# The first pair of x through DRAM and 32-by-32 block transposes, u by one matmul, w from two fp32r halves, in a fused attention and FFN kernel

## The chip, the cores and the metric

The kernel runs on one core of one Trainium2 chip. The metric is the device time of one execution in microseconds, lower is better. The profile is one execution of the program taken by the hardware profiler; its clock starts at the span's start.

## What is computed

Eight sequences of 256 rows and 1024 features, all float32:

```python
x = x + attn(layernorm(x), ctx, Wq, bq, Wk, bk)   # softmax((xn Wq^T + bq)(ctx Wk^T + bk)^T / 32) ctx
x = x + layernorm(x) @ weights + bias             # weights rebuilt from 4-bit codes, scales and zeros
```

The kernel folds the two projections: it makes M = Wq^T Wk once, and then t = xn M for all rows, so that scores are t ctx^T. The biases give two vectors: u = Wk^T bq, which is added to t per column, and w = Wq^T bk, whose product with each row of xn is a term of that row. Float32 products are made of two fp32r halves each (hi and lo, lo = full - hi) with three matmuls: hi hi, hi lo, lo hi.

## The kernel before

All engines run their own written-out programs and meet at semaphores. TensorE's order is: 24 warming transposes, the projection M in eight blocks of 128 rows (`proj(b, c)`, b the block, c the contraction slice, six matmuls of 128x512 each, 48 a block; blocks 0 and 1 are interleaved), then t in four pairs of batches (`for p in range(PAIRS)`, `for j in range(NB)`, n = 8 p + j, 24 matmuls of 128x512 each), with eight `gather` steps of the FFN's tables behind n = 4, 6, 9, 11, 16, 18, 22, 24; then scores, softmax, the product with ctx, and the FFN.

Around each projection block b, ScalarE splits block b + 1 of Wq (`wq_split(b + 1, 0)` after slice 3 of block b has been used, since there is one buffer; `wq_split(b + 1, 1)` after the whole of block b), multiplies block b by bk (`times_bk(b)`, eight instructions) and copies M's hi half (two `m_hi`). VectorE makes the lo halves of the same (`wq_split`, `m_lo`) and sums the products with bk into `wacc` (`sum_bk(b)`). SyncE's queue loads Wq's blocks through three stages: `load_wq(b)` waits until `times_bk(b - 3)` is done.

Layer norm of batches 0 and 1 is on VectorE in blocks 4 and 5: `x_stats` (four bn_stats) and `x_apply` in place in `xin`. In block 7 TensorE transposes them: `x_tr(u)`, four 128x128 float32 transposes of each of eight u into banks 6 and 7, from where ScalarE (`x_hi(0, u)`) and VectorE (`x_lo(0, u)`) write `xT_hi` and `xT_lo` over Wk's halves, once slice 3 of block 7 is used. `u_sums`, behind slice 6 of block 7, sums `uacc` over the partitions with eight float32 matmuls against a column of ones, each two instructions in the trace, and one more for bq bk. `w_row`, behind block 7, sums `wacc` over the partitions with two float32 matmuls of 128x512 (four instructions). ScalarE copies its result four times (`wrow`, `wrow_q`); then VectorE does `row_terms(0)`, `row_terms(1)`, `x_stats(2)`, `x_apply(2)`, `row_terms(2)`, `x_stats(3)`, `x_apply(3)`, `row_terms(3)` and `pick(0)`, which makes the one-hot table that the first gather waits for.

Batches 2 to 7 already take another way: applied rows are written to `xin` with their columns reordered (`by_quadrant`), stored to DRAM in rows of 4 KB (`store_xn`), reloaded in 1 KB pieces so that each 32 partitions hold one quarter of the features (`load_quadrants`, four DMAs on ScalarE's queue), and transposed in place in 32-by-32 blocks by VectorE (`x_blocks`, 128x2048). The first matmul of pair p waits for `x_lo(p, 0)`. For n = 0 the i-th contraction step also waits for the halves of M's block i.

Of the kernel before, what the change touches and what calls it, by code (L numbers as in the profile page):

```python
# [13 lines left out]
P = 128  # L14
# [34 lines left out]
def xattn_ffn_kernel(nc, x, ctx, Wq, bq, Wk, bk, qweight, qzeros, scales, bias, g_idx, out):  # L49
# [21 lines left out]
    with ExitStack() as stack:  # L71
# [49 lines left out]
        qz = at("qz", 200.25, [P, P], I32)  # L121
        KT = QUADRANTS[-1] + G
# [24 lines left out]
        xq = [None] + [at(f"xq{p}", kb, [P, 2 * NB, S], F32) for p, kb in ((1, slot[2]), (2, slot[4]), (3, 162.25))]  # L147
# [11 lines left out]
        xjunk = [at(f"xjunk{t}", 188.25 + 2 * t, [P, D], BF16) for t in range(QT)]  # L159

# [41 lines left out]
        s_const, s_small = sem("constants_made"), sem("small_loaded")  # L202
        s_placed = sem("table_placed")
# [22 lines left out]
        s_xraw, s_xst = [sem(f"raw_x_loaded{i}") for i in range(2)], sem("xn_stored")  # L226
        s_xql = [sem(f"xn_reloaded{i}") for i in range(2)]
        s_xT = sem("xn_transposed_by_blocks")
        s_xtr, s_xhi, s_xlo = sem("xn_transposed"), sem("xT_hi_done"), sem("xT_lo_done")
# [90 lines left out]


# [14 lines left out]
        def _(sp):  # L336
# [88 lines left out]
            def load_raw(b):  # L425
                if b == 2:
                    sp.wait_ge(s_m, 2 * NB)
                elif b == 3:
                    sp.wait_ge(s_xtr, NB)
# [104 lines left out]
        def _(pool):  # L534
# [9 lines left out]

            pool.wait_ge(s_tab[1], 16 * len(QUADRANTS))
# [8 lines left out]
            def rsqrt(n):  # L554
                if n < KH:
                    pool.wait_ge(s_stat, n + 1)
                elif n < B:
                    pool.wait_ge(s_xsq, QT * (n - KH + 1))
                    pool.tensor_scalar(mv[:, :, 1], xsquares, 1.0 / D, EPS, ALU.mult, ALU.add).then_inc(s_xvar, 1)
                    pool.wait_ge(s_xvar, n - KH + 1)  # L560
                else:
                    pool.wait_ge(s_stat, n - B + KH + 1)
                if n < KH:
                    pool.tensor_tensor(rstd, mv[:, :, 1], power, ALU.pow).then_inc(s_rstd, 1)
                else:
                    pool.tensor_tensor(rstd, mv[:, :, 1], power, ALU.pow).then_inc(s_rpow, 1)
                    pool.wait_ge(s_rpow, n - KH + 1)
# [57 lines left out]
        def _(act):  # L625
# [55 lines left out]

            def x_hi(p, u):
                if p == 0:
                    act.wait_ge(s_xtr, u + 1)
                    act.wait_ge(s_wqused, NB)
                    copy(xT_hi[:, u, :], bank[6 + u % 2][:, :]).then_inc(s_xhi, 1)
                else:
                    act.wait_ge(s_xT, 2 * p)
                    if u < NB - 1:
                        act.wait_ge(s_xused, (NB - 1) * (p - 1) + u + 1)  # L690
                    else:
                        act.wait_ge(s_t, NB * p)
                    copy(xT_hi[:, u, :].rearrange("p (m j) -> p m j", j=32), xq[p][:, :, 32 * u:32 * u + 32]
                         ).then_inc(s_xhi, 1)

            for b in range(NB):
# [19 lines left out]
            x_hi(0, 6)  # L716
            x_hi(0, 7)
# [52 lines left out]
            def load_quadrants(b):  # L770
                act.wait_ge(s_xst, 16 * (b - 1))
                if b == B - 1:
# [5 lines left out]

            def x_stats(b):
                act.wait_ge(s_xraw[b % 2], 16 * (b // 2))  # L780
                if b == KH:
                    act.wait_ge(s_placed, 16 * 8)
                    act.wait_ge(s_xn, QT * KH)
                for t in range(QT):
                    act.activation(xjunk[t], raw_rows(b)[:, t, :], ACT.Copy, accum_out=xsum[:, t:t + 1]).then_inc(s_xsum, 1)
                act.wait_ge(s_xsum, QT * (b - KH + 1))
                act.activation(nmean, xsum, ACT.Copy, scale=-1.0 / D).then_inc(s_xmean, 1)
                act.wait_ge(s_xmean, b - KH + 1)
                for t in range(QT):
                    act.activation(xjunk[t], raw_rows(b)[:, t, :], ACT.Square, bias=nmean[:, t:t + 1],  # L790
                                   accum_out=xsquares[:, t:t + 1]).then_inc(s_xsq, 1)

            def x_apply(b):
                act.wait_ge(s_rstd, b + 1)
                act.wait_ge(s_xst, 16 * (b - 2))
                act.wait_ge(s_dot, b)
                for t in range(QT):
                    act.activation(by_quadrant(xin[:, 1, t, :]), raw_rows(b)[:, t, :].rearrange("q (k a i) -> q k a i", k=NB, a=4),
                                   ACT.Identity, bias=shift[:, t:t + 1], scale=rstd[:, t:t + 1]).then_inc(s_xn, 1)
# [128 lines left out]
        def _(dve):  # L928
# [82 lines left out]
            def x_stats(b):  # L1011
                if b < 2:
                    dve.wait_ge(s_xl[b], 16)
                    ln_stats(xin[:, b, :, :])
                else:
                    dve.wait_ge(s_xraw[b % 2], 16 * (b // 2))
                    ln_stats(raw_rows(b))

            def x_apply(b):
                dve.wait_ge(s_rstd, b + 1)  # L1020
                if b == 2:
                    dve.wait_ge(s_xtr, NB)
                elif b > 2:
                    dve.wait_ge(s_xst, 16 * (b - 2))
                for t in range(QT):
                    if b < 2:
                        out_, in_ = xin[:, b, t, :], xin[:, b, t, :]
                    else:
                        out_, in_ = by_quadrant(xin[:, 1, t, :]), raw_rows(b)[:, t, :].rearrange("q (k a i) -> q k a i", k=NB, a=4)
                    dve.tensor_scalar(out_, in_, mv[:, t, 0:1], rstd[:, t:t + 1], ALU.subtract, ALU.mult).then_inc(s_xn, 1)  # L1030

            def x_blocks(b):
                dve.wait_ge(s_xql[b % 2], 64 * (b // 2))
# [3 lines left out]
            def x_lo(p, u):  # L1037
                dve.wait_ge(s_xhi, NB * p + u + 1)
                if p == 0:
                    low(xT_lo[:, u, :], bank[6 + u % 2][:, :], xT_hi[:, u, :], s_xlo)  # L1040
                else:
                    low(xT_lo[:, u, :].rearrange("p (m j) -> p m j", j=32), xq[p][:, :, 32 * u:32 * u + 32],
                        xT_hi[:, u, :].rearrange("p (m j) -> p m j", j=32), s_xlo)

            def copy_u():
                dve.wait_ge(s_u, 1)
                dve.tensor_copy(ucol, bank[4][:, 0:2 * NB].rearrange("p (j two) -> p j two", two=2)[:, :, 0]
                                ).then_inc(s_cons, 1)
                order.link(dve.tensor_copy(bsum[:, 1:2], bank[4][:, 2 * NB:2 * NB + 1]))
# [3 lines left out]
            for b in range(NB):  # L1053
# [13 lines left out]
                if b == NB - 1:  # L1067
                    for u in range(5):
                        x_lo(0, u)
                    copy_u()  # L1070
                    x_lo(0, 5)
# [8 lines left out]
            x_lo(0, 6)  # L1080
            x_lo(0, 7)
# [253 lines left out]
        def _(pe):  # L1335
# [5 lines left out]
            def x_tr(u):  # L1341
                pe.wait_ge(s_xn, 4)
                wait(pe, s_xlo, u - 1)
                for bt in range(2):
                    for t in range(QT):
                        o = bt * S + t * P
                        ins = pe.transpose(bank[6 + u % 2][:, o:o + P], xin[:, bt, t, u * P:(u + 1) * P], ident)  # L1347
                ins.then_inc(s_xtr, 1)

            def u_sums():  # L1350
                pe.wait_ge(s_uacc, NB - 1)
                pe.wait_ge(s_mlo, 2 * (NB - 2))
                for j in range(NB):
                    pe.matmul(bank[4][:, 2 * j:2 * j + 2], uacc[:, j * P:(j + 1) * P], ones2, start=True, stop=True)
                pe.wait_ge(s_cons, 1)
                pe.matmul(bank[4][:, 2 * NB:2 * NB + 2], bsum[:, 0:1].broadcast_to([P, P]), ones2,
# [39 lines left out]
            def w_row():  # L1396
                pe.wait_ge(s_wacc, NB)
                pe.wait_ge(s_cons, 3)
# [191 lines left out]
```

## Time and profile before

| | us |
|---|---|
| median of 3 runs | 547.49 (547.34 to 547.99) |
| the profiled execution | 547.35 |
| its span on the core | 545.6 |
| TensorE busy | 539.3 (99%) |
| VectorE busy | 372.4 (68%) |
| ScalarE busy | 268.0 (49%) |
| GpSimd busy | 187.2 (34%) |

The profiled execution took 547.35, its span 545.6; the other 1.75 lie around it. Matmuls are pipelined, so the duration printed for one (0.39) is longer than the distance to the next; distances between starts are what counts.

### The profile page before, as it was taken

The page shows a single profiled execution, that of the slowest core. Times are in us where ns is not written, and L with a number is a line of the kernel's source. Part 1 is how long each engine was busy: PE and PEld are TensorE (multiplying, and loading weights), DVE is VectorE, ACT ScalarE, POOL GpSimd, SP SyncE. Part 2 cuts the span into 40 slices and gives each one's busy share as a digit, 9 for nine tenths or more (in the row PEclk, how much of TensorE's full clock was granted, in tenths as well). Part 3 has the DMA queues.
Part 4 walks back from the last instruction along what each step waited for, and adds up shares of the span by engine and source line. Part 5 has one row for each costly group of instructions (what it writes and reads, how often), then busy time and mean ns, then how long its engine had stood idle before and what let it go on. Part 6 is the DMA issues. An engine that isn't in the chain of part 4 may idle for free.

```text
span 545.6 us, 7455 instructions
## 1 busy us (share of the span) xinstructions
PE 539.3 (99%) x2686; PEld 452.0 (83%) x2686; DVE 372.4 (68%) x616; ACT 268.0 (49%) x474; POOL 187.2 (34%) x147
## 2 busy tenths in 40 slices
PE   8999999999999999999999999999999999999997
PEld 7888888887777877778898999998788888888886
DVE  4989775787698774793424555574768779778742
ACT  6983444414767582343437766686563243324210
POOL 1072000010011000000326877777756644753530
PEclk9999999999999999999999999999999999999999
DMA  8942100359688756836384899898346775774311
GB/s 270 314 157 79 38 1 0 123 156 313 195 228 292 204 193 193 262 86 192 126 293 144 298 362 355 321 389 346 144 123 244 220 216 203 230 232 134 98 77 77
DMA packets 56036, 108.14 MB, mean 198 GB/s; under 512 B 12000, under 2 KB 32552, under 8 KB 53824
## 3 DMA queue, kind: packets, MB, share of 16 engines
q1 hardware_dynamic: 49472, 101.38, 54.1%
q10 hardware_dynamic: 6528, 6.29, 5.7%
q8 instruction: 21, 0.34, 0.3%
q14 instruction: 15, 0.12, 0.1%
HBM read 67.74 MB, written 39.85 MB: 197 GB/s over the span
## 4 chain that ended last, share of the span: by engine, by line
PE 86%; DVE 4%; ACT 3%; DMA 3%; issue 1%; POOL 1%; ACTq 0%; SPq 0%; DVEq 0%; POOLq 0%
PE bank L1337 22%; PE bank L1339 22%; PE bank L1338 22%; PE bank L1384 5%; PE bank L1390 5%; PE bank L1387 5%; PE bank L1438 2%; DMA xq<-xn_scratch 1%; ACT yin L868 1%; POOL cn_lo L578 1%; DVE xq L1035 1%; DMA wq_stage<-in_L_xattn_Wq 1%; DVE xT_lo L932 1%; PE bank L1347 1%; ACT cn_hi L627 1%
## 5 line engine op out<-in xcount | busy, mean ns | idle before, releaser
L1337 PE MATMUL bank<-xT_hi,m_hi 128*128 128x512 f32 x256 | 101.0, 395 | 0.0
L1339 PE MATMUL bank<-xT_hi,m_lo 128*128 128x512 f32 x256 | 99.7, 390 | 0.0
L1338 PE MATMUL bank<-xT_lo,m_hi 128*128 128x512 f32 x256 | 99.6, 389 | 0.0
L585 POOL TENSOR_TENSOR tT_lo<-t_pair,tT_hi 128x1024 fp32r<-128x1024 f32 x16 | 38.1, 2398 | 75.4 <-ACT tT_hi L627 75.4
L1289 DVE TENSOR_TENSOR xres<-xres,bank 128x512 f32<-128x512 f32 x56 | 38.3, 683 | 36.1 <-PE bank L1339 36.0
L599 POOL TENSOR_TENSOR l_lo_s<-l_sum_s,l_hi_s 128x512 fp32r<-128x512 f32 x32 | 40.4, 1297 | 56.0 <-DVE l_sum_s L1230 56.0
L824 ACT ACTIVATE t_pair<-bank,ucol 128x512 f32<-128x512 f32 x32 | 22.0, 687 | 74.1 <-PE bank L1339 69.6
L1337 PEld LDWEIGHTS bank<-xT_hi,m_hi 128*128 128x128 f32 x256 | 48.0, 188 | 11.8 <-issue 2.1
L1339 PEld LDWEIGHTS bank<-xT_hi,m_lo 128*128 128x128 f32 x256 | 48.0, 188 | 10.2
L1338 PEld LDWEIGHTS bank<-xT_lo,m_hi 128*128 128x128 f32 x256 | 48.1, 188 | 10.0 <-issue 0.2
L1384 PE MATMUL bank<-wk_hi,wq_hi 128*128 128x512 f32 x128 | 50.5, 394 | 0.2 <-DVE wq_lo L932 0.2
L1390 PE MATMUL bank<-wk_hi,wq_lo 128*128 128x512 f32 x128 | 49.9, 390 | 0.0
L1387 PE MATMUL bank<-wk_lo,wq_hi 128*128 128x512 f32 x128 | 49.8, 389 | 0.0
L578 POOL TENSOR_TENSOR cn_lo<-cin,cn_hi 128x512 fp32r<-128x512 f32 x32 | 40.3, 1289 | 26.0 <-ACT cn_hi L627 26.0
L932 DVE TENSOR_TENSOR cT_lo<-bank,cT_hi 128x512 fp32r<-128x512 f32 x32 | 20.7, 686 | 28.6 <-ACT cT_hi L627 28.4
L605 POOL TENSOR_TENSOR xres<-xres,bias_rows 128x1024 f32<-128x1024 f32 x16 | 38.3, 2398 | 0.0
L1337 PE MATMUL bank<-r_tile,l_hi_s 128*128 128x512 f32 x96 | 37.4, 390 | 0.0
L1339 PE MATMUL bank<-r_tile,l_lo_s 128*128 128x512 f32 x96 | 37.4, 389 | 0.0
L1338 PE MATMUL bank<-r_tile,l_hi_s 128*128 128x512 f32 x96 | 37.4, 389 | 0.0
L627 ACT ACTIVATE l_hi_s<-l_sum_s 128x512 fp32r<-128x512 f32 x32 | 20.3, 634 | 34.2 <-DVE l_sum_s L1226 16.2
L1337 PE MATMUL bank<-cT_hi,tT_hi 128*128 128x256 f32 x128 | 36.6, 286 | 0.0
L1339 PE MATMUL bank<-cT_hi,tT_lo 128*128 128x256 f32 x128 | 35.7, 279 | 0.0
(158 smaller groups left out, 1244.0 us busy)
## 6 DMA issues: line engine op xcount, KB each, us to landing
xres<-in_x SPq DMA_DIRECT2D x8, 1024.0 KB, 11.9
out<-xres SPq DMA_DIRECT2D x15, 512.0 KB, 5.2
right_scratch<-part_hi SPq DMA_DIRECT2D x28, 256.0 KB, 2.2
cin<-in_ctx SPq DMA_DIRECT2D x7, 1024.0 KB, 6.1
xn_scratch<-xin SPq DMA_DIRECT2D x6, 1024.0 KB, 4.7
xq<-xn_scratch ACTq DMA_DIRECT2D x24, 256.0 KB, 5.4
r_tile<-right_scratch SPq DMA_DIRECT2D x6, 1024.0 KB, 12.2
yn_scratch<-yin SPq DMA_DIRECT2D x6, 1024.0 KB, 4.0
```

Of the source, the lines that this page charges most:

```text
L578: pool.tensor_tensor(cn_lo[:, kt, cols], cin[b % 3][:, kt, cols], cn_hi[:, kt, cols].bitcast(F32), ALU.subtract).then_inc(s_cnlo, 1)
L585: pool.tensor_tensor(tT_lo[b][:, ks, :], t_pair[b // 2][:, b % 2, ks, :], tT_hi[b % 2 if b else 2][:, ks, :].bitcast(F32), ALU.subtract).t ...
L599: pool.tensor_tensor(l_lo[name], l_sum[name], l_hi[name].bitcast(F32), ALU.subtract).then_inc(s_llo_p, 1)
L605: pool.tensor_tensor(x1_of(f)[:, t, :], x1_of(f)[:, t, :], bias_rows, ALU.add).then_inc(s_rb, 1)
L932: return dve.tensor_tensor(out_, full, hi.bitcast(F32), ALU.subtract).then_inc(done, 1)
L1289: dve.tensor_tensor(part, part, prod_bank(f, n)[:, :], ALU.add).then_inc(s_acc, 1)
L1337: pe.matmul(out_, a_hi, b_hi, start=start, stop=False, skip_group_check=True)
L1338: pe.matmul(out_, a_hi, b_lo, start=False, stop=False, skip_group_check=True)
L1339: return pe.matmul(out_, a_lo, b_hi, start=False, stop=stop, skip_group_check=True)
L1384: pe.matmul(out_, q_hi, wk_hi[:, c, cols], start=c == 0, stop=False, skip_group_check=True)
L1387: pe.matmul(out_, q_hi, wk_lo[:, c, cols], start=False, stop=False, skip_group_check=True)
L1390: ins = pe.matmul(out_, q_lo, wk_hi[:, c, cols], start=False, stop=c == NB - 1, skip_group_check=True)
```

## The change

- `x_stats` and `x_apply` of batches 0 and 1 move from VectorE (blocks 4 and 5) to ScalarE (blocks 3 and 4): two Copy with a sum, the mean, two Square with a sum, GpSimd's rsqrt and shift, two Identity in place. `x_stats` stands between `wq_split(b + 1, 0)` and `times_bk(b)`, `x_apply` behind `wq_split(b + 1, 1)` and ahead of `m_hi(b)`.
- Each batch is stored to DRAM by SyncE's queue as eight DMAs with 128-byte pieces on the SBUF side (`store_first`), and reloaded by four DMAs (`reload_first`). `store_first(0)` stands ahead of `load_wq(7)`; behind that stand `reload_first(0)`, `store_first(1)`, `reload_first(1)`.
- VectorE transposes them by blocks in blocks 6 and 7; `x_hi` and `x_lo` of pair 0 read `xq[0]` as those of other pairs do, all eight ahead of M's block 7. `x_tr` is gone.
- u: VectorE transposes `uacc` by blocks and sums over 32 columns in block 4 (`upart`); one float32 matmul of 32 columns against `same` (ones where partition and column agree modulo 32; made by GpSimd at the start) and the one for bq bk follow, behind slice 6 of block 4.
- w: `wacc` is split into `w_hi` (ScalarE) and `w_lo` (VectorE) at block 7, and `w_row` is four fp32r matmuls of 128x512.

```diff
             for b in range(3, NB):
+                if b == NB - 1:
+                    store_first(0)
                 sp.wait_ge(s_wqlo, wq_split_count(b - 3, 1))
                 sp.wait_ge(s_wqbk, b - 2)
                 load_wq(b)
...
+            reload_first(0)
+            store_first(1)
+            reload_first(1)
...
+            def store_first(b):
+                sp.wait_ge(s_xn, QT * (b + 1))
+                for t in range(QT):
+                    pieces = xin[:, b, t, :].rearrange("p (k a i) -> p a k i", k=NB, a=4)
+                    for a in range(4):
+                        sp.dma_start(xn_dram[b, t * P:(t + 1) * P, a * S:(a + 1) * S].rearrange("p (k i) -> p k i", k=NB),
+                                     pieces[:, a, :, :]).then_inc(s_xst0[b], 16)
+
+            def reload_first(b):
+                sp.wait_ge(s_wklo, NB)
+                sp.wait_ge(s_wkbq, NB)
+                sp.wait_ge(s_xst0[b], 16 * 4 * QT)
+                rows = xn_dram[b].rearrange("(m j) f -> j m f", j=32)
+                for a in range(4):
+                    sp.dma_start(xq[0][32 * a:32 * a + 32, b * NB:(b + 1) * NB, :], rows[:, :, a * S:(a + 1) * S]
+                                 ).then_inc(s_xq0[b], 16)
...
@@ ScalarE
                 elif 1 < b < NB - 1:
                     wq_split(b + 1, 0)
+                    if b in (3, 4):
+                        x_stats(b - 3)
                     times_bk(b)
                     wq_split(b + 1, 1)
+                if b in (3, 4):
+                    x_apply(b - 3)
                 if b == NB - 1:
-                    for u in range(6):
+                    act.wait_ge(s_const, 3)
+                    copy(ones_r, ones2)
+                    act.wait_ge(s_wacc, NB)
+                    copy(w_hi, wacc).then_inc(s_whi, 1)
+                    for u in range(NB):
                         x_hi(0, u)
...
@@ VectorE
-                if b in (4, 5):
-                    x_stats(b - 4)
-                    x_apply(b - 4)
+                if b == KH:
+                    dve.wait_ge(s_uacc, NB - 1)
+                    order.link(dve.transpose(uacc, uacc))
+                    dve.tensor_reduce(upart, uacc.rearrange("p (b i) -> p b i", i=32), AX_X, ALU.add).then_inc(s_upart, 1)
+                if b == 5:
+                    copy_u()
+                if b >= NB - 2:
+                    x_blocks(b - (NB - 2))
...
                 if b == NB - 1:
-                    for u in range(5):
+                    dve.wait_ge(s_whi, 1)
+                    low(w_lo, wacc, w_hi, s_wlo)
+                    for u in range(NB):
                         x_lo(0, u)
...
@@ TensorE
             def u_sums():
-                pe.wait_ge(s_uacc, NB - 1)
-                pe.wait_ge(s_mlo, 2 * (NB - 2))
-                for j in range(NB):
-                    pe.matmul(bank[4][:, 2 * j:2 * j + 2], uacc[:, j * P:(j + 1) * P], ones2, start=True, stop=True)
+                pe.wait_ge(s_upart, 1)
+                pe.wait_ge(s_same, 1)
+                pe.matmul(bank[7][:, 0:32], same, upart, start=True, stop=True)
...
                 for h in range(2):
-                    pe.matmul(bank[4 + h][:, :], ones2[:, 0:1].broadcast_to([P, P]), wacc[:, h * HALF:(h + 1) * HALF],
-                              start=True, stop=True).then_inc(s_wr, 1)
+                    cols = slice(h * HALF, (h + 1) * HALF)
+                    pe.matmul(bank[4 + h][:, :], ones, w_hi[:, cols], start=True, stop=False, skip_group_check=True)
+                    pe.matmul(bank[4 + h][:, :], ones, w_lo[:, cols], start=False, stop=True, skip_group_check=True
+                              ).then_inc(s_wr, 1)
...
                     proj(b, c)
+                    if b == 4 and c == 6:
+                        u_sums()
                     if b == NB - 1:
-                        if c == 6:
-                            u_sums()
-                        for u in {3: (0, 1), 4: (2,), 5: (3, 4), 6: (5,), 7: (6, 7)}.get(c, ()):
-                            x_tr(u)
                         if c == NB - 1:
                             w_row()
```

## Rows read from the trace of the kernel before

**Rows 1.** The page, busy time by engine and TensorE's granted clock in tenths.

```profile
PE 539.3 (99%) x2686; PEld 452.0 (83%) x2686; DVE 372.4 (68%) x616; ACT 268.0 (49%) x474; POOL 187.2 (34%) x147
...
PEclk9999999999999999999999999999999999999999
```

**Rows 2.** TensorE's timeline, end of the projection: start, duration, engine, line, operation, tiles.

```profile
87.92 0.39 PE L1390 MATMUL bank<-wk_hi,wq_lo 128*128 128x512 f32 x1
88.15 1.03 PE L1347 MATMUL bank<-ident,xin 128*128 128x128 f32 x8
...
89.25 0.40 PE L1387 MATMUL bank<-wk_lo,wq_hi 128*128 128x512 f32 x1
...
94.50 1.84 PE L1354 MATMUL bank<-pairs,uacc 128*128 128x2 f32 x16
...
96.42 0.63 PE L1347 MATMUL bank<-ident,xin 128*128 128x128 f32 x4
...
98.29 1.03 PE L1347 MATMUL bank<-ident,xin 128*128 128x128 f32 x8
99.16 1.88 PE L1400 MATMUL bank<-wacc,pairs 128*128 128x512 f32 x4
...
101.11 0.39 PE L1338 MATMUL bank<-xT_lo,m_hi 128*128 128x512 f32 x1
```

**Rows 3.** TensorE's timeline, around the first gather and the start of pair 1.

```profile
127.89 0.39 PE L1339 MATMUL bank<-xT_hi,m_lo 128*128 128x512 f32 x1
128.21 0.39 PE L1426 MATMUL bank<-tab,onehot 32*128 32x512 bf16 x4
...
145.36 0.39 PE L1339 MATMUL bank<-xT_hi,m_lo 128*128 128x512 f32 x1
```

**Rows 4.** ScalarE's timeline: block 3, block 6, then statistics and their application to batch 4.

```profile
44.88 0.63 ACT L627 ACTIVATE wq_hi<-wq_stage 128x512 fp32r<-128x512 f32 x1 [3.53 <-PE bank L1390]
45.42 2.45 ACT L655 ACTIVATE wq_bk<-wq_stage,bcols 128x128 f32<-128x128 f32 x8
...
84.46 2.46 ACT L655 ACTIVATE wq_bk<-wq_stage,bcols 128x128 f32<-128x128 f32 x8
...
101.67 0.62 ACT L627 ACTIVATE uacc<-bank 128x512 f32<-128x512 f32 x1
...
131.72 1.06 ACT L785 ACTIVATE xjunk<-xin 128x1024 bf16<-128x1024 f32 x1 [2.71 <-DMA xin<-in_x]
...
136.47 0.67 ACT L824 ACTIVATE t_pair<-bank,ucol 128x512 f32<-128x512 f32 x1
137.93 2.38 ACT L798 ACTIVATE xin<-xin,shift,pairs 128x1024 f32<-128x1024 f32 x2 [0.78 <-POOL shift L568]
```

**Rows 5.** VectorE's timeline: the last sum_bk, the row terms, pick(0), pair 1's lo halves.

```profile
86.95 1.97 DVE L979 TENSOR_REDUCE wacc<-wq_bk 128x128 f32<-128x1024 f32 x1 [1.43 <-ACT wq_bk L655]
...
102.33 0.69 DVE L1090 CUSTOM_DVE_ANT_0 junk<-xin,wrow 128x512 f32<-128x512 f32 x1 [1.32 <-ACT uacc L627]
...
127.14 0.33 DVE L1105 TENSOR_SCALAR onehot<-gid,pid 128x128 bf16<-128x128 bf16 x1
...
141.07 2.31 DVE L1035 STREAM_TRANSPOSE xq<-xq 128x2048 f32<-128x2048 f32 x1 [7.06 <-DMA xq<-xn_scratch]
...
144.59 4.90 DVE L932 TENSOR_TENSOR xT_lo<-xq,xT_hi 128x512 fp32r<-128x512 f32 x8
```

**Rows 6.** Groups of VectorE instructions by shape: busy us, mean ns, idle before.

```profile
L1035 DVE STREAM_TRANSPOSE xq<-xq 128x2048 f32<-128x2048 f32 x6 | 13.8, 2308 | 13.0 <-DMA xq<-xn_scratch 13.0
L945 DVE TENSOR_TENSOR wk_lo<-wk_stage,wk_hi 128x1024 fp32r<-128x1024 f32 x5 | 6.1, 1223 | 1.5 <-ACT wk_hi L627 1.5
L1193 DVE TENSOR_REDUCE pairs<-bank 128x2 f32<-128x512 f32 x8 | 5.5, 682 | 0.0
```

**Rows 7.** DMA issue timelines, then two-microsecond windows: length, busy by engine, clock, DMA share, GB/s.

```profile
240.23 6.16 SPq L459 DMA_DIRECT2D cq<-in_ctx  x4
...
118.80 1.85 ACTq L776 DMA_DIRECT2D xq<-xn_scratch  x4
...
116.00:118.00 2.00, 2.00 (x11) 1.65 (x10) 1.86 (x8) 0.56 (x1) 0.00 (x0) 1.00 1.01 403
244.00:246.00 2.00, 2.00 (x10) 1.66 (x9) 1.86 (x4) 0.00 (x0) 0.00 (x0) 1.00 0.74 114
246.00:248.00 2.00, 2.00 (x11) 1.65 (x10) 1.21 (x3) 0.60 (x2) 0.00 (x0) 1.00 0.96 151
```

More of the change, by code:

```diff
@@ L121, in xattn_ffn_kernel @@
         qz = at("qz", 200.25, [P, P], I32)
+        same = at("same", 200.75, [P, P], F32)
+        upart = at("upart", 206.5, [P, 32], F32)
+        ones_r = at("ones_r", 206.625, [P, 2], F32R)
+        w_hi = at("w_hi", 196.25, [P, D], F32R)
+        w_lo = at("w_lo", 192.25, [P, D], F32R)
         KT = QUADRANTS[-1] + G
@@ L159, in xattn_ffn_kernel @@
         xjunk = [at(f"xjunk{t}", 188.25 + 2 * t, [P, D], BF16) for t in range(QT)]
+        xjunk_early = [at(f"xjunk_early{t}", 61.75 + 2 * t, [P, D], BF16) for t in range(QT)]
         cn_hi = at("cn_hi", 178.25, [P, QT, D], F32R)
@@ L319, in xattn_ffn_kernel @@
                 LO_AT.setdefault(SUMS[k] + i // 2, []).append((k, i))
+        ON_ACT = {b: i + 1 for i, b in enumerate((0, 1, 4, 5, 6, 7))}
         X_STATS = {1: 3, 5: 4, 10: 5, 12: 6, 17: 7}
@@ L543, in _ @@
             pool.iota(pidi, [[0, 1]], base=0, channel_multiplier=1).then_inc(s_const, 1)
+            order.link(pool.memset(same, 0.0))
+            for d in range(-3, 4):
+                ins = pool.affine_select(out=same, in_=same, compare_op=ALU.not_equal, fill=1.0,
+                                         base=32 * d, pattern=[[-1, P]], channel_multiplier=1)
+                if d < 3:
+                    order.link(ins)
+            ins.then_inc(s_same, 1)
             pool.wait_ge(s_tab[1], 16 * len(QUADRANTS))
@@ L680, in _, with x_stats @@
                 times_bq(c)
+            def x_stats(b):
+                if b < 2:
+                    act.wait_ge(s_xl[b], 16)
+                    rows, places = xin[:, b, :, :], xjunk_early
+                    if b == 0:
+                        act.wait_ge(s_uacc, NB - 1)
+                else:
+                    act.wait_ge(s_xraw[b % 2], 16 * (b // 2))
+                    rows, places = raw_rows(b), xjunk
+                    if b == KH:
+                        act.wait_ge(s_placed, 16 * 8)
+                        act.wait_ge(s_xn, QT * KH)
+                for t in range(QT):
+                    act.activation(places[t], rows[:, t, :], ACT.Copy, accum_out=xsum[:, t:t + 1]).then_inc(s_xsum, 1)
+                act.wait_ge(s_xsum, QT * ON_ACT[b])
+                act.activation(nmean, xsum, ACT.Copy, scale=-1.0 / D).then_inc(s_xmean, 1)
+                act.wait_ge(s_xmean, ON_ACT[b])
+                for t in range(QT):
+                    act.activation(places[t], rows[:, t, :], ACT.Square, bias=nmean[:, t:t + 1],
+                                   accum_out=xsquares[:, t:t + 1]).then_inc(s_xsq, 1)
@@ new lines, in x_apply @@
+            def x_apply(b):
+                act.wait_ge(s_rstd, b + 1)
+                if b >= 2:
+                    act.wait_ge(s_xst, 16 * (b - 2))
+                    act.wait_ge(s_dot, b)
+                for t in range(QT):
+                    if b < 2:
+                        out_, in_ = xin[:, b, t, :], xin[:, b, t, :]
+                    else:
+                        out_, in_ = by_quadrant(xin[:, 1, t, :]), raw_rows(b)[:, t, :].rearrange("q (k a i) -> q k a i", k=NB, a=4)
+                    act.activation(out_, in_, ACT.Identity, bias=shift[:, t:t + 1], scale=rstd[:, t:t + 1]).then_inc(s_xn, 1)
@@ L1011, in x_stats @@
             def x_stats(b):
[L1012 to L1017, printed above, removed]
+                dve.wait_ge(s_xraw[b % 2], 16 * (b // 2))
+                ln_stats(raw_rows(b))
             def x_apply(b):
@@ L1038, in x_lo @@
                 dve.wait_ge(s_xhi, NB * p + u + 1)
[L1039 to L1043, printed above, removed]
+                low(xT_lo[:, u, :].rearrange("p (m j) -> p m j", j=32), xq[p][:, :, 32 * u:32 * u + 32],
+                    xT_hi[:, u, :].rearrange("p (m j) -> p m j", j=32), s_xlo)
             def copy_u():
                 dve.wait_ge(s_u, 1)
-                dve.tensor_copy(ucol, bank[4][:, 0:2 * NB].rearrange("p (j two) -> p j two", two=2)[:, :, 0]
-                                ).then_inc(s_cons, 1)
-                order.link(dve.tensor_copy(bsum[:, 1:2], bank[4][:, 2 * NB:2 * NB + 1]))
+                for a in range(4):
+                    rows = slice(32 * a, 32 * a + 32)
+                    ins = dve.tensor_copy(ucol[rows, :], bank[7][rows, 0:32].rearrange("p (k a) -> p a k", a=4)[:, a, :])
+                ins.then_inc(s_cons, 1)
+                order.link(dve.tensor_copy(bsum[:, 1:2], bank[7][:, 32:33]))
                 dve.sem_inc(s_cons, 1)
```

99 lines of the change are left out of this document (34 added, 65 removed).

## The prediction

> **What bounds the kernel now.** I read busy time by engine first: TensorE is busy 539.3 of 545.6 us at full clock throughout [rows 1], so a microsecond of TensorE work taken out is worth a microsecond only if nobody else becomes late. Next TensorE's own timeline where the change acts. Matmuls of 128x512 start 0.227 us apart: from the second one of t at 101.11 to the last ahead of the first gather at 127.89 there are 118 steps, 26.78 us [rows 2, 3]. So a projection block of 48 takes 10.88 us, and with slice 4 of block 7 due at 88.15 the earlier blocks begin at 50.07 (block 4), 60.95 (5), 71.83 (6) and 82.71 (7). Last I read VectorE's and ScalarE's timelines for where they stand relative to TensorE [rows 4, 5], and this decides the forecast: the first gather (128.21) needs the one-hot table, made from 127.14 to 127.47, only 0.7 us ahead; and the first matmul of pair 1, due 0.227 behind that of 145.36, needs the lo half made from 144.59, ready at 145.28, so 0.1 us or so is spare. Both hang on one chain that starts with VectorE's row terms at 102.33.
>
> **TensorE's work: what goes.** The 24 matmuls left of block 7 would end, and t start, at 88.15 + 5.44 = 93.59. The second matmul of t starts at 101.11, so the first effectively at 100.88. The extras cost 7.3 us by that, or summed from the gaps: eight transposes push the next pair of matmuls by 89.25 - (88.15 + 0.23) = 0.87, that is 0.109 each, 3.5 for 32; the 18 instructions for u 94.50 to 96.42, 1.9; w 99.16 to 100.88, 1.7. Sum 7.1 to 7.3 [rows 2].
>
> **What comes.** w: four fp32r matmuls of 512 columns, 4 x 0.227 = 0.9. u: two float32 matmuls, four instructions at 1.92/18 = 0.107, so 0.43. Net work taken off TensorE: 7.2 - 1.3 = 5.9 us. If TensorE stayed the only bound this would be the gain.
>
> **ScalarE in blocks 3 and 4 (times of the trace of before).** Statistics of a batch cost 4.75 (131.72 to the next instruction at 136.47), an application 2.3 (137.93, two in 2.38 with their overlap) [rows 4]. Block 3: wq_split(4, 0) at 44.88, next 45.42; statistics to 50.17; times_bk(3), 2.35 to the next instruction, to 52.5; wq_split(4, 1) to 53.1; application to 55.4; m_hi(3) to 56.3. Block 4: wq_split(5, 0) to 56.9, statistics to 61.6, times_bk(4) to 63.9, wq_split(5, 1) to 64.5, application to 66.8. VectorE follows: sum_bk(3) 52.6 to 54.55 (as 86.95, 1.97 [rows 5]), lo of wq_split(4, 1) at 55.25. TensorE needs that for slice 4 of block 4 at 55.51: cover of 0.2 us, so a stall of 0 to 0.3, and I take 0.05.
>
> **u on VectorE.** Its transpose and sum come behind m_lo(3) (waits for m_hi(3), so 56.0 to 57.2) and lo of wq_split(5, 0) (to 57.8). No row shows either at this size: the transpose of 2048 columns takes 2.31, a sum of 512 0.68 [rows 6]; for 1024 columns I take 1.2 each by halving and doubling; the ends are 0.7 and 2.0 (sum_bk's strided 1024 [rows 5]) for the sum. So upart is ready at 60.4. TensorE reaches the end of slice 6 of block 4 at 50.07 + 7 x 1.36 + 0.05 = 59.6. It stalls 0.75 (0.2 to 1.6), with everything behind it queued. With 0.05, the work of 0.43 and a drained pipeline of 0.1 TensorE is delta = 1.3 us later than before from block 5 on. Were that stall absent, slice 4 of block 5 would bind instead: its lo half is ready at 66.6 against 66.4 + 0.5, so delta is not under 0.5. With delta = 1.3 this has 1.1 us of cover.
>
> **SyncE's queue.** load_wq(6) now waits for the later times_bk(3): 52.6 instead of 47.9, lands by 57, needed at 67. store_first(0) starts at 55.4 ahead of load_wq(7); that waits for times_bk(4) at 63.9 anyway and lands by 69, needed at 79. How long the store takes is the unknown that matters. 1 MB in 128-byte pieces is moved once in this trace, from DRAM for cq: four issues fill 6.16 us (240.23 to 246.4), with 4.9 from the last issue to landing at most, and the engines carry 114 to 151 GB/s then against 403 for xn in 4 KB rows [rows 7]. So the ends are 4.7 (as the 4 KB rows) and, in the other direction, an unknown above the 9.6 of cq; I take 9.6, the same piece size. A reload takes 1.85 of issue and some 5.4 to land, 7.3 [rows 7]. Then: store(0) 55.4 to 65, reload(0) to 72.4 (needed at 80), store(1) from 67, sharing with the reload, to 79.5, reload(1) to 86.8. VectorE asks for it at 88.86 + 1.3 = 90.2. Hidden, with 3.4 us of cover. load_raw(2) behind it waits for block 7's end, later than that.
>
> The Trainium skill speaks against this edit: "DMA: Bandwidth & Descriptors", in its opening table, says that transfers need 512 B or more for line rate because the engine below that does a read-modify-write. The cq row agrees in direction, 114 to 151 against 403 GB/s, but it reads DRAM in small pieces; no row of before writes DRAM in them. By the row the change is hidden; by the rule taken as a doubling for writes it is the slower rival below.
>
> **The end of the projection: VectorE and ScalarE become the bound.** All plus delta. times_bk(7) starts at 84.46, sum_bk(7) at 86.95 and frees VectorE at 88.86 [rows 4, 5]. x_blocks(1) 2.24 to 91.1; w_lo 1.1 (1.22 with overlap [rows 6]) to 92.2; eight x_lo 4.85 (4.90 [rows 5]) to 97.1; two m_lo to 98.3. ScalarE meanwhile: x_hi from 91.2, eight at 0.525, to 95.4; m_hi to 96.4; four copies of w's row 2.05 (the last of the four at 101.67 ends at 102.29 [rows 4]) to 98.45. So row_terms(0) starts at 98.5 + delta instead of 102.33. TensorE starts t at 93.6 + 0.9 + delta = 94.5 + delta, and its eight steps of n = 0 find x_lo and m_lo ready (last needed 99.3, ready 98.3). So against TensorE VectorE is 2.6 us later than before: 4.0 behind the start of t, where it was 1.45.
>
> **What is late next.** The chain from the row terms to pick(0) is VectorE's own work, 127.47 - 102.33 = 25.1. The one-hot comes at 98.5 + 1.3 + 25.1 = 124.9; TensorE is at the gather at 94.5 + 1.3 + 27.3 = 123.1. Stall 1.8. From the row terms hangs also x_apply(3), its store, the reload and VectorE's transpose at 141.07, which waited 7.06 for that DMA [rows 5]: pair 1 then starts later by another 0.7 or so. Together TensorE in pair 1 stands where this chain puts it: 102.33 - 99.8 = 2.5 earlier than before, and 0.1 more for the spare. Behind pair 1 nothing changes and everything keeps its distance to TensorE. Gain 2.6: span 543.0, execution 547.35 - 2.6 = 544.75, and the median of runs is 0.14 above the profiled one: **544.9**.
>
> **Rivals.**
> 1. *The 128-byte stores are dear.* Landing of batch 1 is 64.6 + 2 T + about 3, T the time of one store, since the second waits for the first. From T = 11.3 the cover is gone, from 12.5 the whole gain; each microsecond more costs two. At T = 16 it lands at 99.6, 9.4 late: 554. For it: no row of before writes 128-byte pieces. Against: cq's 9.6. By the skill's rule above this is the outcome.
> 2. *TensorE stays the bound*: x_hi, x_lo and row terms are less late than I say. Then 5.9 less the stalls of 0.8: 542.4. Against it is the 0.7 us of cover at the first gather; it needs two microseconds of slack that I don't find.
> 3. *The covers are a little thinner*: u's sum at 2.0, slice 4 of block 4 late by half a microsecond, or T near 12. Gain 0 to 1: 547. Nothing excludes it; each cover is 0.2 to 3.4 us wide.
>
> **Numbers.** Forecast 0.58 with its own range 543.5 to 546.3 (delta from 0.5 to 2.6 and the chain); rival 1 0.19; rival 2 0.09; rival 3 0.14. A measurement of this kernel tells 0.2%, 1.1 us, from no change. Faster is forecast and rival 2, 0.67; same is rival 3, 0.14; slower is rival 1, 0.19. The range for 8 in 10 takes in the forecast, most of rival 2, rival 3 and the near part of rival 1: 542.4 to 549.
>
> **What would show it.** Right: TensorE idle 0.6 to 0.9 us ahead of u's matmul near 59.6 on upart; 1.5 to 2 us at the first gather on onehot; row terms at 99.8; pair 1 some 2.6 us earlier than before. Wrong: VectorE's second transpose waiting for the reload (rival 1), no wait at the gather (rival 2), waits at slice 4 of blocks 4 or 5 (rival 3).

## The result and the profile after

The changed kernel takes 546.42 us, median of 16 executions (544.53 to 547.63), against 547.64 (547.21 to 548.22, 16 executions) of the kernel before: ratio 0.9974, 95% interval 0.9966 to 0.9982. It is faster by 1.4 us in the ratio and 1.2 in the medians, where 2.6 was forecast. The executions of the kernel before lie within 1.0 us, those of the changed one within 3.1: that spread is the first thing to explain. The mean granted clock of each execution divides them: seven of the 16 have 0.997 and take 546.71 to 547.63, nine have 0.999 or 1.0 (full clock, from here on) and take 544.53 to 546.63, median 545.68.

Two profiled executions of the changed kernel are used, because they differ. The first has a span of 545.1 at a mean granted clock of 0.997 (called *after*), the second 542.8 at 1.0 (called *after again*; the same code, profiled beside the experiments). The forecast span was 543.0.

TensorE's waits of *after again*: engine, line, what it waited for, us in total, times, longest.

```profile
PE bank L1472 <- DVE onehot L1160: 1.8, 1, 1.8
PE bank L1407 <- POOL pairs L574: 1.5, 1, 1.5
PE bank L1399 <- DVE upart L1113: 0.5, 1, 0.5
```

The wait on upart (0.75 forecast) and the 1.8 on the one-hot table (forecast to a tenth) are there; before there was neither. VectorE's timeline of the same execution, from the last sum_bk to the row terms:

```profile
88.22 1.99 DVE L1036 TENSOR_REDUCE wacc<-wq_bk 128x128 f32<-128x1024 f32 x1 [1.42 <-ACT wq_bk L696]
90.13 2.30 DVE L1088 STREAM_TRANSPOSE xq<-xq 128x2048 f32<-128x2048 f32 x1
92.35 1.18 DVE L989 TENSOR_TENSOR w_lo<-wacc,w_hi 128x1024 fp32r<-128x1024 f32 x1
93.45 4.90 DVE L989 TENSOR_TENSOR xT_lo<-xq,xT_hi 128x512 fp32r<-128x512 f32 x8
98.27 1.28 DVE L989 TENSOR_TENSOR m_lo<-bank,m_hi 128x512 fp32r<-128x512 f32 x2
99.69 0.69 DVE L1145 CUSTOM_DVE_ANT_0 junk<-xin,wrow 128x512 f32<-128x512 f32 x1
```

The block transpose at 90.13 shows no wait, so the reload had landed. The row terms start at 99.69, forecast 99.8, before 102.33 [rows 5]. Then the one-hot table and the transpose that waits for the reload of batch 3:

```profile
124.52 0.33 DVE L1160 TENSOR_SCALAR onehot<-gid,pid 128x128 bf16<-128x128 bf16 x1
...
137.32 2.31 DVE L1088 STREAM_TRANSPOSE xq<-xq 128x2048 f32<-128x2048 f32 x1 [5.93 <-DMA xq<-xn_scratch]
```

And TensorE at the first gather, *after again*; the last matmul ahead of it is at 122.78, the gather at 125.00, against 127.89 and 128.21 before [rows 3]:

```profile
122.78 0.39 PE L1394 MATMUL bank<-xT_hi,m_lo 128*128 128x512 f32 x1
125.00 0.40 PE L1472 MATMUL bank<-tab,onehot 32*128 32x512 bf16 x4 [1.83 <-DVE onehot L1160]
```

So TensorE reaches the gather 5.1 us earlier and leaves it 3.2 us earlier; 2.8 us are left at the end of the span. That is the forecast's sum, in one execution at full clock (544.66), which is among the fastest of its kind. Now the other profile, *after*, same place: windows of two microseconds with length, busy time by engine, granted clock, DMA share and GB/s.

```profile
124.00:126.00 2.00, 0.50 (x5) 0.30 (x6) 1.75 (x7) 0.42 (x1) 0.00 (x0) 1.00 1.03 377
126.00:128.00 2.00, 2.00 (x7) 1.55 (x8) 2.00 (x1) 0.00 (x0) 0.00 (x0) 0.75 1.02 412
128.00:130.00 2.00, 2.00 (x6) 1.62 (x5) 1.97 (x5) 0.60 (x1) 0.00 (x0) 0.50 1.03 418
130.00:132.00 2.00, 2.00 (x9) 1.61 (x9) 1.82 (x3) 1.94 (x6) 0.00 (x0) 0.90 1.03 327
```

The third number from the end is the clock: TensorE stood idle for 1.8 us, took up work, and was then granted 0.50, that is 1.2 instead of 2.4 GHz. In TensorE's timeline the distance between matmuls goes from 0.23 to 0.43:

```profile
126.63 0.40 PE L1392 MATMUL bank<-xT_hi,m_hi 128*128 128x512 f32 x1
126.86 0.49 PE L1393 MATMUL bank<-xT_lo,m_hi 128*128 128x512 f32 x1
...
129.29 0.63 PE L1393 MATMUL bank<-xT_lo,m_hi 128*128 128x512 f32 x1
129.71 0.63 PE L1394 MATMUL bank<-xT_hi,m_lo 128*128 128x512 f32 x1
130.14 0.52 PE L1392 MATMUL bank<-xT_hi,m_hi 128*128 128x512 f32 x1
130.50 0.39 PE L1393 MATMUL bank<-xT_lo,m_hi 128*128 128x512 f32 x1
```

From 127.15 to 130.14 seven distances of 0.427 take 3.0 us instead of 1.6. Where *after again* and *after* are 0.5 us apart at the gather, the eviction behind the first step of pair 1 comes at 147.99 in one and 150.11 in the other, 2.1 apart: the half clock cost 1.6 us. No wait in the list of waits shows it.

### The profile page after: what moved, and what is told of

Same layout as the page of the kernel before. It is cut to its first block, busy times and chain, and to the rows that moved or that the text cites. A ratio compares the mean times of both kernels' runs of the same rounds, so it can differ in the third digit from the quotient of the medians.

```text
span 545.1 us, 7417 instructions
## 1 busy us (share of the span) xinstructions
PE 536.2 (98%) x2640; PEld 449.9 (83%) x2640; DVE 372.0 (68%) x606; ACT 282.4 (52%) x498; POOL 190.5 (35%) x159
## 4 chain that ended last, share of the span: by engine, by line
PE 77%; DVE 10%; ACT 7%; DMA 2%; issue 2%; POOL 1%; ACTq 0%; DVEq 0%; POOLq 0%
PE bank L1392 21%; PE bank L1394 20%; PE bank L1393 20%; PE bank L1429 4%; PE bank L1432 4%; PE bank L1435 4%; PE bank L1484 2%; DVE junk L1145 2%; DVE xq L1088 1%; DMA right_scratch<-part_hi 1%; DMA xq<-xn_scratch 1%; PE bank L1407 1%; DVE stats L1057 1%; POOL cn_lo L619 1%; ACT yin L925 1%
```

## The experiments

Two theories of where the missing half of the gain went. A: TensorE's idle time at the first gather, made by VectorE's later chain, brings the half clock in part of the executions. B: the half clock, or the spread, comes from something else of the change (its stores, ScalarE's work, the start). Times are medians of the device time beside the kernel before on the same chip.

### The changed kernel once more, the one-hot table early, the wait filled, u later

These four ran together; the kernel before took 547.89 (546.74 to 548.60) in 18 executions.

The changed kernel as it is:

> The changed kernel as it is, beside the others. In its first profile TensorE waited 1.8 us for the one-hot table ahead of the first gather (123.5 to 125.5), then ran at half clock for about 4 us, and began block 0 0.9 us later than the kernel before. Theory A (the wait is VectorE's chain, the half clock follows from it): the 1.8 us wait is there again, the half clock in some executions and not in others, median 546.4. Rival B (start-up differs by chance, no link): the wait is there, the half clock is not tied to it.

Measured: 546.37 (544.40 to 548.05, 12 executions), ratio 0.9971 (0.9957 to 0.9984). The wait is there, this profile has no half clock: the same 1.8 us of idle time bring it in one execution and not in the next. Six of the twelve executions have 0.997 (546.72 to 548.05, median 547.10), six the full clock (544.40 to 546.01, median 545.02).

The one-hot table made ahead of time:

```diff
                 if b == 3:
                     tables()
+                    dve.tensor_scalar(onehot[0], gid...[:, nibble(0), :], pid[:, 0:1], None, ALU.is_equal).then_inc(s_oh, 1)
...
             def pick(i):
-                dve.tensor_scalar(onehot[i % 2], gid_t[:, t, :], pid[:, 0:1], None, ALU.is_equal).then_inc(s_oh, 1)
+                if i > 0:
+                    dve.tensor_scalar(onehot[i % 2], gid_t[:, t, :], pid[:, 0:1], None, ALU.is_equal).then_inc(s_oh, 1)
```

> One part moved: the one-hot table of the first gather is made in block 3, behind the tables, instead of behind the row terms. Theory A (VectorE's chain from the row terms to the one-hot holds TensorE back by 1.8 us, and the half clock follows from that idle time): the wait at the first gather is gone, no half clock, and TensorE stops next for at most 0.8 us at the first lo half of pair 1 (ready near 141.7 in the trace of the changed kernel); 1.1 us faster than the changed kernel's clean executions and 2 us faster than its median, 544.4. Rival (TensorE is bound elsewhere and the wait is only moved): the same 1.8 us are waited for at pair 1, time as the changed kernel's clean executions, 545.5.

Measured: 544.66 (544.06 to 545.32, 5 executions), ratio 0.9945 (0.9932 to 0.9958), 1.7 faster than the changed kernel. All five are at full clock. The wait at the gather is gone; the next is the one of pair 1, longer than the 0.8 that was expected:

```profile
PE bank L1395 <- DVE xT_lo L989: 1.3, 1, 1.3
```

The wait filled with work that nobody reads:

```diff
                 if i == 0:
                     pe.wait_ge(s_placed, 16 * 8)
                     pe.wait_ge(s_wrow, 2)
                     pe.wait_ge(s_xlo, NB)
+                    for m in range(16):
+                        pe.transpose(bank[6][:, m % 4 * P:(m % 4 + 1) * P], ident, ident)
                 pe.wait_ge(s_oh, i + 1)
```

> The changed kernel with 16 float32 transposes of the identity into bank 6 (1.75 us of TensorE work that nobody reads) put into the wait ahead of the first gather. Nothing else moves. Theory A (the granted clock falls because TensorE stands idle there): the clock stays full in every execution, the gather comes at the same time, median 545.6 (0.8 below the changed kernel). Rival B (the clock falls for another cause, as the DMA load of that stretch): the half clock is still seen in some executions, the median is that of the changed kernel or a little above it.

Measured: 544.52 (544.32 to 544.89, 5 executions), ratio 0.9943 (0.9931 to 0.9955). This is the decisive run. TensorE does 1.75 us more, the one-hot table is no earlier (124.71), and the median is 1.85 us lower, all five executions at full clock and within 0.6 us of each other and of the fastest of the changed kernel (544.40). More work on an engine that is busy 99% of the time made the kernel faster in the median, since it took the place of idle time. Against the full-clock profile of the changed kernel nothing is won: the gather is at 125.11 instead of 125.00, the span 542.7 instead of 542.8. VectorE, from the timeline of this kernel:

```profile
124.71 0.33 DVE L1160 TENSOR_SCALAR onehot<-gid,pid 128x128 bf16<-128x128 bf16 x1
```

The gain is larger than the 0.8 us expected, and the half clock isn't all of it. Between the means of *after_ref* and *fill_gather* there are 1.7 us (546.20 and 544.54). The six executions at full clock have a mean of 545.14, so 1.1 of the 1.7 come with the half clock. The other 0.6 lies between executions at full clock; what it is, no run shows.

The two matmuls for u later:

```diff
-                    if b == 4 and c == 6:
+                    if b == 5 and c == 2:
                         u_sums()
```

> The two matmuls for u moved from behind slice 6 of block 4 to behind slice 2 of block 5; nothing else moves. Theory A (everything behind block 4 is shifted by the 0.5 us that TensorE waits for upart, VectorE's chain too): that wait is gone, row terms and first gather come 0.5 us earlier, slice 4 of block 5 waits not at all or at most 0.1; 0.5 us faster than the changed kernel, 545.9. Rival (the stall is absorbed in the wait at the first gather): that wait becomes 2.3 us and the time is unchanged.

Measured: 545.18 (544.07 to 547.00, 7 executions), ratio 0.9955 (0.9940 to 0.9971). The wait on upart is gone, the row terms start at 99.02 (99.69 in *after again*, of which 0.2 is an earlier start of the projection), the wait at the gather is still 1.8. So the half microsecond reaches the row terms and isn't absorbed in that wait, as theory A has it. At the end of the kernel it isn't settled: the profiled span is 542.3, 0.5 under *after again*, with the 0.2 of the start in it, and the medians are 1.2 apart with both spreads at 3 us. Two of the seven executions have 0.997.

### The same idle time in the kernel before, and the same filled

If theory A holds, the kernel before must show the effect too. Only VectorE's table is made late:

```diff
                 wait(dve, s_g, i - 1)
+                if i == 0:
+                    for _ in range(7):
+                        order.link(dve.tensor_copy(junk, wrow[:, 0:HALF]))
                 dve.tensor_scalar(onehot[i % 2], gid_t[:, t, :], pid[:, 0:1], None, ALU.is_equal
```

> The kernel before with seven copies of 128x512 (2.5 to 3 us of VectorE, read by nobody) ahead of the one-hot table of the first gather, so that TensorE waits there 1.8 to 2.3 us; pair 1 doesn't hang on it, since VectorE has 7 us idle ahead of it. Nothing of the change is in it. Theory A (TensorE's idle time there costs itself and, in some executions, a stretch at half clock): clean executions 1.8 to 2.3 us over the kernel before, others up to 2 us more, so a spread of about 3 us and granted clocks of 0.997 among them. Rival (the half clock comes from something else in the change, as the 128-byte stores or ScalarE's extra work): all executions 2 us over the kernel before with its spread of under 1.5 us.

Measured: 550.49 (550.11 to 552.22, 6 executions) against 547.76 (547.10 to 549.00, 13 executions), ratio 1.0057 (1.0042 to 1.0072). The copies take 3.2 us and the wait is 2.6, somewhat more than expected. Four executions lie at 550.1 to 550.5 with full clock, two at 551.8 and 552.2 with 0.997, and the one of the latter that was profiled shows the half clock with nothing of the change in the kernel. Windows of its trace:

```profile
128.00:130.00 2.00, 0.65 (x3) 0.19 (x1) 1.86 (x5) 0.69 (x1) 0.00 (x0) 1.00 1.00 360
130.00:132.00 2.00, 0.78 (x5) 0.38 (x6) 1.90 (x5) 0.19 (x1) 0.00 (x0) 0.76 0.99 401
132.00:134.00 2.00, 2.00 (x5) 1.58 (x6) 2.00 (x2) 2.00 (x4) 0.00 (x0) 0.50 1.03 398
```

Then the same with 22 transposes in the wait, written as in the run above:

> before_gap with 22 float32 transposes of the identity (2.4 us) on TensorE in its wait at the first gather. Theory A (idle time, not the lateness of the table, brings the half clock): the gather comes at the same time, the clock stays full, median 550.3 with a spread of under 1.2 us, no execution above 551.2. Rival (the half clock has to do with the stretch itself): executions of 551.8 to 552.2 as in before_gap.

Measured: 550.15 (549.64 to 550.46, 5 executions) against 548.00 (547.58 to 548.38, 9 executions), ratio 1.0041 (1.0028 to 1.0055). The gather is as late behind its last matmul, no execution is above 550.5, all five are at full clock. Five executions against two in six would be thin by themselves; all runs together are not. In the kernels whose profile has a wait of TensorE of 1.8 us or more behind the start (the changed kernel, *u_late*, *before_gap*, and *double_store* below), 22 of 47 executions have a mean granted clock of 0.996 or 0.997. In the eight others with an edit, whose longest such wait is 1.3, none of 42 has, and none of the 49 of the kernel before beside them. In each of the three profiles with 0.996 or 0.997, the one stretch under full clock stands at such a wait. So B falls as the cause of the half clock: neither the change's stores nor the stretch of the kernel brings it, the idle time does. The spread that is left among executions at full clock it does not explain.

### The stores of the first batches

```diff
                         sp.dma_start(xn_dram[b, t * P:(t + 1) * P, a * S:(a + 1) * S].rearrange("p (k i) -> p k i", k=NB),
                                      pieces[:, a, :, :]).then_inc(s_xst0[b], 16)
+                        if b == 1:
+                            sp.dma_start(spare_dram[t * P:(t + 1) * P, a * S:(a + 1) * S].rearrange(...),
+                                         pieces[:, a, :, :]).then_inc(s_xst0[b], 16)
```

> The changed kernel with each of the eight stores of batch 1 issued twice, the second time to a spare tensor, and both waited for. In the changed kernel the reload lands near 88 and VectorE asks for it at 90.7. Theory (2.7 us of cover, then one for one): the store takes 8 to 13 us more, the second block transpose waits 5 to 10 us, and the time rises by 5 to 9 us over the changed kernel, 551 to 556. Rival (the end of the projection doesn't hang on the store): no change.

Measured: 549.24 (548.39 to 550.07, 6 executions), ratio 1.0025 (1.0013 to 1.0037), 2.9 over the changed kernel. SyncE's queue in *after again*, then here; the reload of batch 1 is the last line of the first and the first line of the second.

```profile
55.45 5.09 SPq L391 DMA_DIRECT2D xn_scratch<-xin  x8
...
66.82 11.00 SPq L391 DMA_DIRECT2D xn_scratch<-xin  x8
80.54 1.80 SPq L400 DMA_DIRECT2D xq<-xn_scratch  x4
```

```profile
86.69 1.80 SPq L404 DMA_DIRECT2D xq<-xn_scratch  x4
...
93.78 2.31 DVE L1092 STREAM_TRANSPOSE xq<-xq 128x2048 f32<-128x2048 f32 x1 [3.38 <-DMA xq<-xn_scratch]
```

Another megabyte in 128-byte pieces delays the reload by 6.2 us, the transpose waits 3.4: the difference, 2.8, is the cover, as read. The expected 5 to 9 us missed because the added store cost 6 us and not 8 to 13. Rival 1 of the prediction has its mechanism shown here, with its first microseconds; in the changed kernel it does not come to pass. TensorE waits 2.0 us for w_lo, from 95 to 97, and here too the clock falls behind the idle time (0.56 from 98 to 100); five of the six executions have 0.996 or 0.997. The wait, and that window:

```profile
PE bank L1451 <- DVE w_lo L993: 2.0, 1, 2.0
```

```profile
98.00:100.00 2.00, 2.00 (x6) 1.51 (x6) 2.00 (x4) 2.00 (x5) 0.00 (x0) 0.56 0.77 317
```

### Behind the first gather: the wait of pair 1

```diff
-        RAW = {2: (4, 5), 6: (6,), 12: (7,)}
+        RAW = {2: (4,), 6: (5, 6), 12: (7,)}
```

on top of the early one-hot table.

> onehot_early, and the load of raw batch 5 (1 MB) moved from the third step of pair 0 to the seventh, behind the reload of batch 3. With onehot_early TensorE waited 1.3 us at pair 1 for the first lo half, whose block transpose waited 6.4 us for the reload of batch 3, which shares the DMA engines with two raw loads. Theory A (contention with that load delays the reload by 3 to 4 us): the transpose starts near 134.5, the wait at pair 1 is gone, 1.3 us faster than onehot_early, 543.3. Rival (the reload is late for its own issue, or the wait moves on to raw batch 5): same time or slower, with ScalarE waiting for raw batch 5 near 150.

Measured: 543.10 (542.71 to 544.62, 6 executions) against 547.76, ratio 0.9921 (0.9908 to 0.9935). The wait at pair 1 is gone, and VectorE's transpose comes at 134.70 instead of 137.97:

```profile
134.70 2.31 DVE L1088 STREAM_TRANSPOSE xq<-xq 128x2048 f32<-128x2048 f32 x1 [3.80 <-DMA xq<-xn_scratch]
```

It is 4.3 us under the kernel before by its ratio; the two variants of it below, *combined* and *same_late*, are as fast (0.9918 and 0.9916), and these numbers don't tell the three apart. With u later as well:

> raw5_late with the two matmuls for u behind slice 2 of block 5 as in u_late. Theory A (with no wait left between block 4 and pair 1 all three parts add up): 0.4 to 0.5 us faster than raw5_late, 542.9, 5 us under the kernel before, near to the 5.9 us of TensorE work that the change takes out. Rival (another chain of VectorE becomes late once TensorE is 5 us earlier, as the gather of step 9 or pair 2): no faster than raw5_late, with a new wait of TensorE on VectorE between 140 and 240.

Measured: 543.59 (542.30 to 544.10, 6 executions), ratio 0.9918 (0.9904 to 0.9932): no faster than without. Its profile has TensorE waiting 0.9 us for a weight tile at the last gather (0.5 in raw5_late) and 0.2 for a lo half, so part of what is won ahead is given back there, as its rival has it; a part of its profiled span is the start (below). How much is due to which can't be told by these numbers.

### w again from float32

```diff
-                    pe.matmul(bank[4 + h][:, :], ones, w_hi[:, cols], start=True, stop=False, skip_group_check=True)
-                    pe.matmul(bank[4 + h][:, :], ones, w_lo[:, cols], start=False, stop=True, skip_group_check=True
-                              ).then_inc(s_wr, 1)
+                    pe.matmul(bank[4 + h][:, :], ones2[:, 0:1].broadcast_to([P, P]), wacc[:, cols],
+                              start=True, stop=True).then_inc(s_wr, 1)
```

> One part of the change undone: w is summed again by two float32 matmuls of 128x512 from wacc, without w_hi and w_lo. TensorE gets 0.8 to 0.9 us of work back ahead of t. Theory A (behind the projection VectorE's and ScalarE's chain sets the time, so TensorE's saving on w is spent in the wait at the first gather): the row terms start within 0.3 us of where they did (ScalarE's copies of w's row still end last, x_hi and the block transpose stay ahead), the wait at the gather shrinks from 1.8 to about 1.0, clean executions as the changed kernel's (544.5), and with less idle time fewer or no executions at half clock, median 544.5 to 545.5. Rival (TensorE's work counts): 0.8 slower than the changed kernel, 547.2.

Measured: 545.69 (544.61 to 546.17, 5 executions), ratio 0.9955 (0.9942 to 0.9967). The wait at the gather is 1.0 instead of 1.8, the row terms start at 99.80, and the kernel is not slower: by the medians 0.7 faster, its slowest execution 1.9 below that of the changed kernel. All five executions are at full clock; beside those of the changed kernel at full clock (median 545.6 of 15) it is the same. So as the change stands its part on w buys nothing, and by making TensorE idle longer it costs those executions that fall to the half clock.

```profile
PE bank L1465 <- DVE onehot L1155: 1.0, 1, 1.0
```

> raw5_late with the same part undone. There TensorE waits for nobody between block 4 and the last gather. Theory A (with the waits gone TensorE is the bound and its work counts one for one): 0.8 slower than raw5_late, 543.9. Rival (w's part is worth nothing anywhere): 543.1.

Measured: 544.58 (544.22 to 544.72, 5 executions) against 548.00, ratio 0.9937 (0.9925 to 0.9950). By the ratios it is 0.9 us slower than raw5_late, as expected where TensorE is the bound, though the two intervals overlap. The same edit is worth nothing in one kernel and, as far as these intervals tell, 0.9 us in the other.

### The start

> raw5_late with GpSimd's matrix same made near 44 us, behind the tables, instead of from 3 to 8 us. In twelve looks TensorE's first projection matmul started at 5.4 to 5.8 us (3 of 3 of the kernel before and its variants, 4 of 10 of the changed kernel and its variants) or at 6.3 to 6.5 (6 of 10). Theory (chance, nothing in TensorE's start waits for GpSimd's work on same): median and spread as raw5_late, 543.1 and 542.7 to 544.6. Rival (GpSimd's work at the start slows TensorE's warming): the first matmul starts under 5.8 us, all executions under 543.5, median 542.6.

Measured: 543.64 (542.53 to 543.73, 5 executions), ratio 0.9916 (0.9901 to 0.9931). The first matmul of the projection starts at 6.54: the rival falls, GpSimd's work on `same` has nothing to do with it. Timelines of this kernel and of raw5_late:

```profile
1.51 5.38 PE L1410 MATMUL bank<-ident 128*128 128x128 f32 x24 [1.51 <-POOL pairs L574]
6.54 0.78 PE L1432 MATMUL bank<-wk_hi,wq_hi 128*128 128x512 f32 x1
```

```profile
1.51 4.16 PE L1410 MATMUL bank<-ident 128*128 128x128 f32 x24 [1.51 <-POOL pairs L574]
5.42 0.48 PE L1432 MATMUL bank<-wk_hi,wq_hi 128*128 128x512 f32 x1
```

The same 24 warming transposes take 5.4 us in one execution and 4.2 in another. Of these 1.1 us at the first projection matmul 0.8 are left at the last sum_bk (88.81 against 87.98) and 0.9 between the spans (541.8 and 540.9). It isn't always so: *w_fp32* also starts at 6.54 and has its last sum_bk at 88.30, 0.1 behind *after again*, which starts at 5.70. *after* (6.54) against *before* (5.63) has 0.9 at the start, and what reaches block 3 is 0.6 (ScalarE's wq_split(4, 0) at 45.46 against 44.88 [rows 4]).

Whether the change has a part in the later starts is open. The three profiles without it start at 5.6 to 5.8; of the eleven with it four start at 5.4 to 5.7 and seven at 6.3 to 6.5. Three are too few to say, and no run but this one looks for a cause. Late and early starts may be what spreads the executions at full clock; that isn't shown either.

## Why the prediction was right, and where it was short

- **TensorE's work.** Taken off: 7.2, put back 1.3. t begins in *after again* at 95.80; forecast 95.8, before 100.88 [rows 2]. Right.
- **ScalarE's and VectorE's order in blocks 3 to 5.** A wait of 0.5 for upart instead of 0.75, none at slice 4 of blocks 4 and 5. Right; the sum over 1024 columns took 1.22, as doubled.
- **SyncE's queue.** The second store starts at 66.8 (67 forecast) and the reload at 80.5 (79.5); cover 2.8 (3.4). The cover is right, its terms less so. By the windows of *after again* (166, 189 and 173 GB/s from 56 to 62, then 4) the first store took some 6.5 us where 9.6 was put; the second, beside the reload, took 13.7 from its start to the reload's issue where 12.5 was put. The 166 to 189 GB/s are more than the 114 to 151 of reading cq in 128-byte pieces and less than half of the 403 of the 4 KB rows [rows 7]. The Trainium skill, "DMA: Bandwidth & Descriptors", in the table at its opening, says that the engine does a read-modify-write below 512 B. The trace agrees in direction; a doubling against cq, which would have been rival 1, did not come.
- **The end of the projection.** Row terms at 99.7, forecast 99.8; one-hot at 124.5, wait 1.8. Right, w_fp32 and raw5_w_fp32 show what it means: TensorE's work isn't the bound there.
- **"What is late next" is the step that failed, in two terms of opposite sign.** It charged the wait with its own length alone. The half clock behind it costs 1.6 us in *after*, and it comes in 13 of the 28 executions of the changed kernel. And the step let pair 1 start later by another 0.7 with a reload as slow as before; the reload landed 1.2 us sooner than that (137.3), there is no wait at pair 1 in *after again*, and its first step of pair 1 is evicted 3.25 us earlier than before (147.99 against 151.24), where 2.6 was forecast. 0.4 of this is lost again by the end of the span (2.8); where, wasn't traced. The 15 executions at full clock have a median of 545.6, 0.7 over the forecast of 544.9, and only the fastest are at it or under it (544.4 to 544.9); what holds the others back is open. The 13 at 0.997 have 546.9. Together they give 546.4, 1.5 over the forecast, just outside the likeliest case's own range and inside the stated one. That the two terms of this step have opposite signs is luck.
- **The rivals.** Dear stores: mechanism shown, not in effect. TensorE as the bound: not so here, and nearly so in raw5_late, whose 4.3 are most of the 5.9. Thinner covers: its gain of 0 to 1 is near the measured 1.2 to 1.4, but no cover failed; the cause is another, which no rival named.

## What to carry to other kernels

Where one engine is busy 99% of the time, taking work off it creates idle time on it, and the idle time can have a price beyond its length (here in 22 of 47 executions with a wait of 1.8 us or more): look where it will stand, and put the producer ahead (here one instruction of 0.33 us moved into an idle stretch of VectorE) or put off what shares its DMA engines. A kernel whose executions suddenly spread over 3 us, where those of the kernel before stay within 2, and part of which have a mean granted clock of 0.997, shows that; a trial with filler work in the wait tells it from a longer chain. And before an edit on the bounding engine is kept, ask in which version of the schedule it is still the bound: the two halves of w were worth nothing until the waits behind them were gone.

## What the runs showed of the hardware

- A wait of TensorE of 1.8 to 2.6 us, with dense work on both sides, was followed in 22 of 47 executions by a lower mean granted clock, and in the three of these that were profiled by a stretch at 0.50 (1.2 GHz). By the windows it began about at the wait's end in *before_gap* (131.0, the gather at 131.22), 1.0 us behind it in *double_store* and 1.5 behind it in *after*, where it cost 1.6 us. With the same 1.8 us *after again* and *u_late* kept full clock in their profiles. Waits of 0.5 us at upart were followed by no such stretch in any profile, nor were those of 1.0 in *w_fp32* and of 1.3 in *onehot_early* and *double_store*.
- The 24 transposes at the start took 4.4 to 4.5 us in the three profiles without the change and 4.2 to 5.4 in the eleven with it.
- Storing 1 MB from SBUF in 128-byte pieces into 1 KB runs of DRAM was issued in 5.1 us with nothing else in SyncE's queue, at 166 to 189 GB/s in the windows behind it, and in 11.0 beside a reload.
